# Three PSUM banks for the grams and four shared ones, in a DLRM top tower

## What is computed

```python
e = stack([tbl_0[ids[:, 0]], ..., tbl_25[ids[:, 25]]], axis=1)
combined = concatenate([dense_output[:, None, :], e], axis=1)      # 2048 x 27 x 128
interactions = einsum('bfd,bgd->bfg', combined, combined)
z = concatenate([dense_output, interactions[:, iu, ju]], axis=1)   # upper triangle: 351 columns
h = concatenate([z, dense_output], axis=1)                         # 607 columns
h = maximum(h @ W_top1 + b_top1, 0.0)                              # 512
h = maximum(h @ W_top2 + b_top2, 0.0)                              # 256
y = h @ W_top3                                                     # 2048 x 1
```

## Time and profile before

| | |
|---|---|
| runs | 563.34, 563.65, 564.11 us; median 563.65 us |
| span of the profiled execution | 563.2 us (this is the one time that is told of it; its distance to the median is 0.45 us) |
| instructions | 9906 |
| busy: TensorE matmul, weight load | 409.3 us, 375.3 us |
| busy: VectorE, ScalarE, GpSimd | 251.8 us, 142.7 us, 258.4 us |
| mean granted TensorE clock | 0.839 of full |

### The profile page before, as it was taken

The page is one execution under the profiler, slowest core; times in us unless marked ns, Lnnn a source line. Parts: engine busy times, 40 slices in busy tenths (PEclk is TensorE's granted clock), DMA queues, the critical chain, the costliest instruction groups (busy, mean ns, idle before and its releaser), DMA issues.

```text
span 563.2 us, 9906 instructions
## 1 busy us (share of the span) xinstructions
PE 409.3 (73%) x4248; PEld 375.3 (67%) x4248; DVE 251.8 (45%) x340; ACT 142.7 (25%) x370; POOL 258.4 (46%) x280
## 2 busy tenths in 40 slices
PE   2477564759785696875859468595885848868998
PEld 1466564759583694875849368585885748857987
DVE  4579243844431654353444344445442354424322
ACT  3263111422121221221122121222221222212431
POOL 6736363553626536262554625546063662625200
PEclk9868695969887698787979689798797968879899
DMA  7954521231212212031212212222121221211000
GB/s 186 246 129 104 178 62 43 61 80 39 57 29 76 74 45 56 25 91 43 56 48 60 68 44 57 47 55 74 25 66 38 72 61 35 65 34 48 21 11 1
DMA packets 20132, 36.73 MB, mean 65 GB/s; under 512 B 6157, under 2 KB 9877, under 8 KB 20090
## 3 DMA queue, kind: packets, MB, share of 16 engines
q0 software_dynamic: 8704, 17.84, 12.4%
q1 hardware_dynamic: 5338, 9.08, 6.3%
q10 hardware_dynamic: 6048, 9.18, 6.2%
HBM read 36.07 MB, written 0.01 MB: 64 GB/s over the span
## 4 chain that ended last, share of the span: by engine, by line
PE 58%; issue 16%; another core or an unknown queue 16%; DVE 6%; ACT 3%; DMA 1%; SPq 0%; DVEq 0%; ACTq 0%
PE psB L424 19%; PE psG L450 15%; PE psB L499 7%; PE psB L506 5%; PE psB L408 5%; DVE one_hot L724 3%; PE psB L493 2%; DVE tab_lo L736 2%; PE psB L511 1%; ACT ET L627 1%; DMA oidx<-hot_idx 1%; PE psB L478 1%; PE psB L475 1%; ACT ET L647 1%
## 5 line engine op out<-in xcount | busy, mean ns | idle before, releaser
L349 POOL DMA_INDIRECT E<-tbl,gidx x272 | 257.5, 947 | 266.3 <-PE psB L408 156.3
L724 DVE TENSOR_TENSOR one_hot<-oidx,psR 125x1024 fp32r<-125x1024 int32 (+1 forms) x152 | 178.0, 1190 | 189.5 <-remote 135.7
L450 PE MATMUL psG<-ET 128*52 128x52 f32 x2048 | 93.3, 263 | 79.1 <-issue 55.7
L450 PEld LDWEIGHTS psG<-ET 128*52 128x52 f32 x2048 | 84.2, 175 | 88.8 <-issue 76.0
L424 PE MATMUL psB<-one_hot,tab_hi 125*128 125x256 f32 x592 | 112.5, 314 | 24.3 <-ACT tab_hi L594 10.9
L424 PE MATMUL psB<-one_hot,tab_lo 125*128 125x256 f32 x592 | 104.5, 300 | 7.2 <-issue 5.1
L424 PEld LDWEIGHTS psB<-one_hot,tab_hi 125*128 125x128 f32 x592 | 89.8, 208 | 29.6 <-issue 20.9
L424 PEld LDWEIGHTS psB<-one_hot,tab_lo 125*128 125x128 f32 x592 | 89.3, 207 | 7.8 <-issue 4.9
L627 ACT COPY ET<-psB 128x512 f32<-128x512 f32 (+3 forms) x80 | 44.2, 570 | 86.6 <-PE psB L408 34.6
L772 DVE COPY_PREDICATED S<-second,psG 116x208 f32<-116x208 int32 x64 | 25.1, 391 | 76.5 <-ACT S L656 76.5
L656 ACT COPY S<-psG 116x208 f32<-116x208 f32 x64 | 21.3, 333 | 103.2 <-remote 52.5
(11 more groups left out here) (54 smaller groups left out, 213.4 us busy)
## 6 DMA issues: line engine op xcount, KB each, us to landing
oidx<-hot_idx ACTq DMA_DIRECT2D x28, 256.0 KB
E<-tbl,gidx POOLq DMA_INDIRECT x272
ET<-tbl SPq DMA_DIRECT2D x3, 448.0 KB
oidx<-hot_idx SPq DMA_DIRECT2D x4, 256.0 KB
dense<-dense_pairs SPq DMA_DIRECT2D x8, 128.0 KB
ZH<-tbl SPq DMA_DIRECT2D x2, 448.0 KB
S<-tbl SPq DMA_DIRECT2D x2, 448.0 KB
oidx<-hot_idx ACTq DMA_DIRECT2D x7, 128.0 KB
```

What stands on the lines that cost most here:

```text
L349: nc.gpsimd.indirect_dma_start(E[:, n % SLOTS, i, :], None, gathered[feature_and_tile(n, i)[0]], bass.IndirectOffsetOnAxis(ap=gidx[:, 4 * ...
L450: gram = nc.tensor.matmul(psG[g % 2][q * LANE:q * LANE + M, a * M:(a + 1) * M], two[:, 0:M], two[:, PAIR:], start=True, stop=True)
L724: nc.vector.tensor_tensor(one_hot[0:ROWS_P, m % RING, 0:many], ids, rows, ALU.is_equal).then_inc(hot_full[m % RING], 1)
```

## The change

The grams get three banks, the other steps share four. Everything that counted modulo 2 counts modulo `G_BANKS`, and `place_fills` deals with four banks. Instructions, their order on each engine and their sizes stay the same, but for one more memset in `clear_G`; what moves is the bank of each fill, and with it what the fill waits for. The pieces of tables at the start stay in the first two gram banks. All lines from L45 on move down by one.

```diff
-    BANKS = 5
+    G_BANKS = 3
+    BANKS = 4
...
-        psG = [pb(f"psG{i}", [P, 512], f32) for i in range(2)]
+        psG = [pb(f"psG{i}", [P, 512], f32) for i in range(G_BANKS)]
...
-                wait_count(pe, G_out[g % 2], g // 2)
+                wait_count(pe, G_out[g % G_BANKS], g // G_BANKS)
...
-                    for g in (gram_number(d, G_FILLS - 2), gram_number(d, G_FILLS - 1)):
-                        pe.wait_ge(G_out[g % 2], g // 2 + 1)
+                    for g in range(gram_number(d, G_FILLS - G_BANKS), gram_number(d, G_FILLS)):
+                        pe.wait_ge(G_out[g % G_BANKS], g // G_BANKS + 1)
...
-                    pe.wait_ge(G_cleared, 2)
+                    pe.wait_ge(G_cleared, G_BANKS)
```

More of the change, by code:

```diff
@@ L286, in dlrm_program @@
         bank_full, bank_out = sems("bank_full", BANKS), sems("bank_out", BANKS)
-        G_full, G_first, G_out = sems("G_full", 2), sems("G_first", 2), sems("G_out", 2)
+        G_full, G_first, G_out = sems("G_full", G_BANKS), sems("G_first", G_BANKS), sems("G_out", G_BANKS)
         G_cleared = sem("G_cleared")
@@ L449, in gram_fill @@
                         two = ET[:, tile % ET_RING, j, q].rearrange("p f s -> p (f s)")
-                        gram = nc.tensor.matmul(psG[g % 2][q * LANE:q * LANE + M, a * M:(a + 1) * M],
+                        gram = nc.tensor.matmul(psG[g % G_BANKS][q * LANE:q * LANE + M, a * M:(a + 1) * M],
                                                 two[:, 0:M], two[:, PAIR:], start=True, stop=True)
-                gram.then_inc(G_full[g % 2], 1)
+                gram.then_inc(G_full[g % G_BANKS], 1)
             def turn_columns(d, b):
                 if b == 0:
-                    for g in (gram_number(d, G_FILLS - 2), gram_number(d, G_FILLS - 1)):
-                        pe.wait_ge(G_out[g % 2], g // 2 + 1)
+                    for g in range(gram_number(d, G_FILLS - G_BANKS), gram_number(d, G_FILLS)):
+                        pe.wait_ge(G_out[g % G_BANKS], g // G_BANKS + 1)
                 bank, full = wait_empty(pe, ("C", d, b))
@@ L537, in gram_samples @@
         def gram_samples(g, q):
-            return psG[g % 2][0:MT, 0:G_SIZE * M].rearrange("p (a f s) -> p f a s", a=G_SIZE, s=PAIR)[:, :, :, q]
+            return psG[g % G_BANKS][0:MT, 0:G_SIZE * M].rearrange("p (a f s) -> p f a s", a=G_SIZE, s=PAIR)[:, :, :, q]
         def gram_rows(d, i):
@@ L654, in empty_gram_first @@
                 g = gram_number(d, i)
-                act.wait_ge(G_full[g % 2], g // 2 + 1)
-                nc.scalar.copy(gram_rows(d, i), gram_samples(g, 0)).then_inc(G_first[g % 2], 1)
+                act.wait_ge(G_full[g % G_BANKS], g // G_BANKS + 1)
+                nc.scalar.copy(gram_rows(d, i), gram_samples(g, 0)).then_inc(G_first[g % G_BANKS], 1)
             def round_pairs(d, i):
@@ L769, in empty_gram @@
                 g = gram_number(d, i)
-                dve.wait_ge(G_first[g % 2], g // 2 + 1)
+                dve.wait_ge(G_first[g % G_BANKS], g // G_BANKS + 1)
                 mine = second[0:MT, :].bitcast(i32).unsqueeze(2).to_broadcast([MT, F - 1, G_SIZE])
-                nc.vector.copy_predicated(gram_rows(d, i), mine, gram_samples(g, 1)).then_inc(G_out[g % 2], 1)
+                nc.vector.copy_predicated(gram_rows(d, i), mine, gram_samples(g, 1)).then_inc(G_out[g % G_BANKS], 1)
             def split_pairs(d, i):
```

## The result

| | before | with the change |
|---|---|---|
| runs | 20, median 563.81 us (560.24 to 566.63) | 20, median 566.2 us (563.38 to 568.36) |
| span of the profiled execution | 563.2 us | 561.4 us |
| TensorE matmul busy | 409.3 us | 408.2 us |
| mean granted clock | 0.839 | 0.842 |

The ratio is 1.0044, with a 95% interval from 1.0026 to 1.0061: slower by 0.4%, about 2.4 us, and clear of the noise. I had forecast no change and 563.4 us, 0.2 us less than before; 566.2 lies inside the range and next to the slower rival's 566.3. In all tables medians are over every run, while ratios and intervals leave out runs more than 1.5% above the kernel's fastest, which matters only for the kernels with row numbers in SBUF. The two spans alone would tell the opposite, because one execution scatters by more than the effect: the profiled run of the change took 563.42 us, near the low end of its 20.

The account below looks back on a forecast made before the run. TensorE's work in program order plus its pauses was taken as the bound. Third gram bank -1.4, pass 6 +0.96 and pass 0 +0.2 gave -0.24 us from the 563.65 us median: 563.4 us, range 561.8 to 567.0.

Parts of the forecast that it names:

- the slower rival: Column stages of passes 1 to 5: pauses hang on TensorE, so delays cost 2.85 us more, 566.3 us; chance 0.30.
- the products at 111.31: Pass 0 table products wait for a bank ScalarE empties at 114.73; cost 0 to 0.4 us, taken as 0.2.
- have over 1 us between the emptying of the bank and their start and lose nothing: Most shared-bank fills outside the column stage: slack over 1 us, so four shared banks cost them nothing.
- something that follows the load and not TensorE's work: Passes 1 to 5, pause after the table products: ended by something behind ScalarE's index load, so TensorE's delays are covered.
- The distance from index load to table copy: On ScalarE, 11.55 us in pass 1 and 11.48 in pass 2; claimed to stay at 11.5 us within 0.1.
- Passes 1 to 5, costed at nothing: Column stages: table products 0.35 or 0.9 us late, covered by 3.6 to 5.7 us of pause, cost nothing.
- Pass 6, +0.96 us: Last column stage: table products 0.96 us late for a bank, with no pause to cover it, so fully paid.
- The third gram bank, -1.4 us: Gram fills: all five waits for emptied gram banks go, gaining 1.4 us, between nothing and 1.8 us.
- the lower end that I had given: Third gram bank: gain of nothing, if each removed wait is followed by a pause of other origin.
- the 0.45 us around the span stay: Whole run: the 0.45 us around the profiled span of 563.2 us, against the 563.65 us median, stay.
- Its clock: Slower rival's second price: TensorE's clock drops after the held column stage, up to 4.1 us more, reaching 567.0 us.
- Running ahead: Rival: third gram bank allows one more fill per "issue" pause, -5.4 us, 558 us, likelier 561.6 us; chance 0.07.

Follow-up runs that it names:

- the kernel that has it alone: Kernel before (two gram banks, five shared) with the shared fills of half passes 0 to 2 limited to four banks: ratio 1.0047.
- early split: W1's weight-split steps moved one half pass forward; with the change's three gram and four shared banks, ratio 1.0000 to the kernel before.
- G3 B4: Three gram and four shared banks, the change run again against the kernel before: ratio 1.0040.
- G2 B5: Two gram and five shared banks, the kernel before written with the changed kernel's constants and run again: ratio 1.0012.
- G2 B4: Changed kernel set to two gram and four shared banks, the eighth bank unused, against the kernel before: ratio 1.0044.
- G3 B5: Three gram and five shared banks, row numbers in SBUF instead of PSUM, against the kernel before: 548.33 us, 0.9664; run again 541.35 us, 0.9668.

## Why the prediction was wrong

**The step that failed** is "Pass 0: the products at 111.31 now wait for a bank that ScalarE empties [...] between 0 and 0.4, I take 0.2". I looked for late banks in the column stage only, since the other fills "have over 1 us between the emptying of the bank and their start and lose nothing". In pass 0 that is false for one fill: `("hot", 1, 12)` gets the bank of W1's second piece (of the first piece before the change), and VectorE's split of it is still running. Its own wait is 1.29 us, and it turned two rows of 8 gathers into 4 and 12, behind which TensorE stood 10.60 us. Much of that replaces pauses that had stood elsewhere in the stage (3.52 us before the transposes at 115.81, for one), and the matmuls ahead of it ran faster (0.66 us for those four transposes, 1.09 in the earlier trace rows). The term was 0.2 us and should have been 1.3 us by the two traces' stretches, or 2.6 us by the ratio 1.0047 of the kernel that has it alone (whose stretch is 2.2 us longer). The upper bound of 0.4 us was no bound, as it came from the rows of one place. The wait that the term was made of did not come at all: the products that were at 111.31 are now at 110.64, and the ScalarE copies that they depend on start at 109.89, not at 114.34. It did come in the kernel with the early split and G3 B4, and there it moved the transposes behind it by 1.2 us, not by 0.4 or less.

**The reason behind it**: I had the pauses ended by "something that follows the load and not TensorE's work", and so nothing that TensorE did late could cost. The distance from index load to table copy, said to stay at 11.5 us within 0.1, is 11.51 us in pass 2 but 10.90 us in pass 1 (184.45 to 195.35), and in pass 0 it went from 7.4 to 15.1 us. It was no constant of the kernel before either: in the trace of G2 B5 it is 10.81 us in pass 1, and in the very trace that I read 10.87 us in pass 5. The load was a companion. What the pause follows is the end of the row of gathers, and its length is set by the moments at which TensorE's transposes free slots. So TensorE's lateness can cost by steps: nothing that could be measured in passes 1 to 5, and over 1 us in pass 0, where it splits a row.

**Passes 1 to 5, costed at nothing: right.** The kernel with four banks from half pass 3 on gives 0.9996, with the delays in its trace (6.3 and 6.4 us from first column block to products in passes 2 and 4, 5.3 and 5.4 before). They are covered, as argued, though not by what I named.

**Pass 6, +0.96 us: right** in the rows, 1.03 us measured; in the time of that same kernel it can't be told, since its interval reaches 1.4 us upward. **The third gram bank, -1.4 us: right in the rows, too large in the time.** The waits for L772 are gone and the last gram stages are 0.30 us shorter each; but G3 B4 against G2 B4 is 1.0040 against 1.0044. The early waits are followed by a pause of other origin, the lower end that I had given. With 0 for the gain, 1.0 for pass 6 and 1.3 to 2.6 for pass 0 the sum would be 2.3 to 3.6 us, against 2.4 measured. That is no proof of the 1.0: the two kernels that have four banks in pass 6 but no row of 12 in pass 0 come out at 0.9996 and 1.0000, and without it the sum is 1.3 to 2.6 us.

**The base**: "the 0.45 us around the span stay" was wrong. In every run with a span beside its time, the time is 1.8 to 2.1 us over the span (563.42 against 561.4, 562.76 against 560.8). So the execution behind the page of before took some 565.2 us, an estimate from these, above the median; it moves no term of the difference.

**The rivals.** The slower rival had nearly the right time for the wrong place: its column stages of passes 1 to 5 cost nothing, as the kernel with four banks there shows. Its clock did not come either: 0.842 against 0.839. The rule of the Trainium skill, "TensorE: Matmul & The Clock Gate", section "A second HAM failure mode: psum-queue depth-cycling", which made it the likelier, was not borne out. Yet its core, "the pauses hang on TensorE after all", is what happened in pass 0. Running ahead: "issue" before L451 is 58.0 us, against 55.7, so no. The rule of the Trainium skill, "Perfetto Trace Analysis", section "Matmul Optimizations", that all 8 banks be used, gave 0 for the sum, and missed the same thing as I did; G2 B4, which leaves a bank unused, is at 1.0044 like the change.

## What to carry to other kernels

Before a deal of shared buffers is costed, look at every fill's new predecessor, the ones from set-up work that is done once above all: here the loss came and went with the wait of one fill behind a one-off weight split. Where an engine issues in rows whose length depends on when slots come free, a delay need not have a price per microsecond; ask whether it splits a row. And a change of buffers is worth what the next bottleneck makes of it: the same one gave +0.4% on this kernel and about -1% after one tensor had moved from PSUM to SBUF, so it is worth trying again when something else has changed.

## What I had not expected of the hardware

- With three of four gathers left out, the time fell from 563 to 365 us and the granted clock rose from 0.842 to 1.000, although TensorE's matmuls are the same. In the kernel before, 29 of ScalarE's 31 waits of over 3 us for "remote" end 1.0 to 3.6 us after the last gather of a row.
- A VectorE operation that reads both its inputs from SBUF makes the gathers beside it slower (1.75 and 1.88 us, against 0.94; 1149 ns in the mean, against 948), and with it the kernel was faster, 0.9860 with nothing else changed. That slow gathers let TensorE's signals through fits this ("remote" before the one-hot builds falls from 126.5 us in the change to 64.5 us with G3 B5), but was not tested by itself.
- Three shared banks were not measurably slower than four: 1.0022 (0.9996 to 1.0049) against 1.0044 (1.0019 to 1.0069).
